# GpSimd adds both halves of the attention mask in every fourth step, TensorE none

## The chip, the cores and the metric

One core of one Trainium2 chip runs the kernel. The metric is the device time of one execution in microseconds (us). Engines in the profile: PE is TensorE's matmul stream and PEld its weight loads, DVE is VectorE, ACT is ScalarE, POOL is GpSimd, SP is SyncE.

## The reference, cut to what matters

`x` is 4096x256, `neigh` 4096x256, `adj` 4096x4096 integers, of which all but a few per row are 0. The output is `x` plus the two halves below.

```python
h = jnp.maximum(_layernorm(x, axis=-1), 0.0)
neib_att = jnp.tanh(neigh @ Wn1 + bn1) @ Wn2 + bn2      # 4096x32
value = neigh @ Wv + bv                                  # 4096x128
x_att = jnp.tanh(h @ Wx1 + bx1) @ Wx2 + bx2              # 4096x32
ws = x_att @ neib_att.T                                  # 4096x4096
ws = jax.nn.leaky_relu(ws, negative_slope=0.01)
ws = jnp.where(adj > 0, ws, -9e15)
agg_neib = jax.nn.softmax(ws, axis=1) @ value
x = x + jnp.concatenate([h @ Wfx + bfx, agg_neib], axis=1)
```

## The kernel before, in words

After a first part that computes `neib_att` and starts `value`, the attention runs in 128 steps. A step s is one chunk of scores: 128 rows of `x` by 1024 neighbours (two PSUM banks of 512). Four chunks make the 4096 neighbours of a tile of rows, four tiles (16 steps) make a group of 512 rows; there are 8 groups. "The step at 5 of a group" is one with s % 16 = 5. Each engine has its own program, written out step by step, and runs it in order; semaphores tie them. The steps of one chunk:

- VectorE, `mask_of` (L680): turns 1024 columns of `adj` into a bf16 mask of 0 or -2^53, two steps ahead, in a ring of three.
- TensorE, `score` (L921, L922): for each half of 512 columns, a matmul of the identity with the mask (L921, which writes the mask into PSUM) and then the matmul of the scores on top of it (L922). From step 19 on (`POOL_MASKS`) the second half has no mask matmul. Before its first matmul it waits for the mask and for `leaked`, the leak of step s - 2, whose PSUM banks it overwrites (L910 to L912).
- ScalarE, `rise` (L552): relu of 99 times the chunk, from PSUM to SBUF.
- GpSimd, in `step` (L438 to L443): from step 19 on, after `rise`, adds the second half of the mask (512 columns) to that result in SBUF.
- VectorE, `leak` (L709): waits for `risen` and `masked`, then adds PSUM and SBUF, times 0.01, which is the leaky relu plus a large negative number where masked, and keeps the running maximum. It is done in VectorE's step s + 1.
- ScalarE, `power` (L564): the exponential of two chunks at once, every second step.

The other half of every step works on the group before, whose weights are ready: two blocks per step, each turned by TensorE (`turn`, L945), copied out rounded by ScalarE (`hi`, L525), its rest computed by VectorE (`lo`, L691), and multiplied with `value` in three matmuls (`product`, L964 to L966). TensorE's `turn` and `product` wait for `lo` of the step before.

The order within a step: TensorE runs both score halves, turn 0, product, turn 1, side work, product. VectorE runs leak(s - 1), lo 0, side work, lo 1, mask_of(s + 2). ScalarE runs hi 0, rise, hi 1, power. GpSimd runs in even steps the load of two chunks of `adj` (`load_adj`, L407, which first waits for VectorE's `mask_done`), then the bias sums of the output (L358, L351), then the mask's add, then the reciprocal root of the variance of the next rows in small operations of 4 columns (`rstd_of`, L369 to L386; steps at 12, 13 and 15 of a group) and their normalisation (`x_normalise`, L391; one each in the steps at 1 and 2, two in the step at 4).

```python
def step(s):            # VectorE, L770
    if s < POOL_MASKS:
        mask_of(s + 2)
    leak(s)             # of chunk s - 1
    lo(s, 0)
    ...
    lo(s, 1)
    if POOL_MASKS <= s < STEPS - 2:
        mask_of(s + 2)
```

Of the kernel before, what the change touches and what calls it, by code (L numbers as in the profile page):

```python
# [29 lines left out]
ALU = mybir.AluOpType  # L30
# [6 lines left out]
BANK = 512  # L37
GROUP = BANK
TILES = GROUP // P
GROUPS = N_X // GROUP  # L40
NEIGH_GROUPS = N_NEIGH // GROUP
CHUNK = 2 * BANK
# [12 lines left out]
MASK_RING = 3  # L55
# [28 lines left out]
V_START, V_STRIDE = 0, 2  # L84
LEFT_0 = 3
POOL_MASKS = BACK_LAG
WARM_UP = 15
NEWTON = 3
NEWTON_OPS = 2 + 4 * NEWTON
# [2 lines left out]
def build(nc, x, adj, neigh, wx1, bx1, wx2, bx2, wn1, bn1, wn2, bn2, wv, bv, wfx, bfx, out):  # L92
    with ExitStack() as ctx:
        def sb(name, shape, dt):
            return ctx.enter_context(nc.sbuf_tensor(name, shape, dt))

        def sem(name):
            return ctx.enter_context(nc.semaphore(name))


        scores = sb("scores", [P, 2 * TILES, N_NEIGH], FP32)
# [4 lines left out]
        mask = sb("mask", [P, MASK_RING, CHUNK], BF16)  # L106
# [90 lines left out]
        masked = sem("masked")  # L197
# [21 lines left out]
        def x_due(s, stage):  # L219

            e = (s - stage) // GSTEPS + 1
            return e if (s - stage) % GSTEPS == 0 and 1 <= e < GROUPS else 0
# [10 lines left out]
        def right_due(s):  # L233

            b = s - FIN_LAG - X_RIGHT
            return b // GSTEPS + 1 if b >= 0 and b % GSTEPS == 0 and b // GSTEPS < GROUPS - 1 else None

        def chunk_of(s):

            return s // GSTEPS % 2, s // CHUNKS % TILES, s % CHUNKS  # L240
# [97 lines left out]
        def _(pool):  # L338
# [8 lines left out]
            def left_sum(e, h):  # L347

                pool.wait_ge(x_left_in, 16 * (e + 1))
                half = x_left.rearrange("p (t d) -> p t d", d=D_OUT)[:, h * TILES // 2:(h + 1) * TILES // 2]  # L350
                pool.tensor_tensor(half, half, b_fx[:, :, :].to_broadcast([P, TILES // 2, D_OUT]), ALU.add).then_inc(  # L351
                    x_summed, 1)

            def right_sum(g, h):

                pool.wait_ge(x_right_in, 16 * (g + 1))
                half = x_right[:, h * TILES // 2:(h + 1) * TILES // 2, :]
                pool.tensor_tensor(half, half, b_v[:, :, :].to_broadcast([P, TILES // 2, D_OUT]), ALU.add).then_inc(  # L358
                    right_summed, 1)

            def rstd_of(e, i):

                done = NEWTON_OPS * e
                if i == 0:
                    pool.wait_ge(aggr_done, e + 1)
                    wait(pool, x_normed, TILES * e)
                    wait(pool, newton, done)
                    pool.sem_inc(pool_joined, 1)
                    pool.tensor_scalar(var_eps[:, :], mean_var[:, :, 1], EPS, None, ALU.add).then_inc(newton, 1)  # L369
                    pool.wait_ge(newton, done + 1)  # L370
                    pool.sem_inc(pool_joined, 1)

                    pool.tensor_scalar(rstd.bitcast(INT32)[:, :], var_eps.bitcast(INT32)[:, :], -0.5,
                                       float(0x5f3759df), ALU.mult, ALU.add).then_inc(newton, 1)
                else:

                    done = done + 2 + 4 * (i - 1)
                    pool.wait_ge(newton, done)
                    pool.tensor_tensor(factor[:, :], rstd[:, :], rstd[:, :], ALU.mult).then_inc(newton, 1)
                    pool.wait_ge(newton, done + 1)  # L380
                    pool.tensor_tensor(factor[:, :], factor[:, :], var_eps[:, :], ALU.mult).then_inc(newton, 1)
                    pool.wait_ge(newton, done + 2)
                    pool.sem_inc(pool_joined, 1)
                    pool.tensor_scalar(factor[:, :], factor[:, :], -0.5, 1.5, ALU.mult, ALU.add).then_inc(newton, 1)
                    pool.wait_ge(newton, done + 3)
                    pool.tensor_tensor(rstd[:, :], rstd[:, :], factor[:, :], ALU.mult).then_inc(newton, 1)  # L386

            def x_normalise(e, i):
                pool.wait_ge(newton, NEWTON_OPS * (e + 1))
                pool.sem_inc(pool_joined, 1)  # L390
                pool.tensor_scalar(x_rows[:, i, :], x_rows[:, i, :], mean_var[:, i, 0:1], rstd[:, i:i + 1],  # L391
                                   ALU.subtract, ALU.mult).then_inc(x_normed, 1)
# [6 lines left out]
            def load_adj(n):  # L399

                tile, c = n // CHUNKS, n % CHUNKS
                if ADJ_RING <= n < ADJ_RING + FRONT:
                    to, ready = adj_front[:, n - ADJ_RING:n - ADJ_RING + LOAD, :], front_ready[(n - ADJ_RING) // LOAD]
                else:
                    i = n % ADJ_RING
                    to, ready = adj_in[:, i:i + LOAD, :], adj_ready[i // LOAD]
                pool.dma_start(to.rearrange("p a n -> p (a n)"),  # L407
                               adj[tile * P:(tile + 1) * P, c * CHUNK:(c + LOAD) * CHUNK]).then_inc(ready, 16)
# [18 lines left out]
            def step(s):  # L427
                n = s + ADJ_RING + (FRONT if s < FRONT else 0)
                if s % LOAD == 0 and n < STEPS and not FRONT <= s < ADJ_RING + FRONT:
                    pool.wait_ge(mask_done, s + LOAD)  # L430
                    load_adj(n)
                for i in range(2):
                    if (g := right_due(s - i)) is not None:
                        right_sum(g, i)
                for i in range(2):
                    if e := x_due(s, X_SUM[i]):
                        left_sum(e, i)
                if POOL_MASKS <= s < STEPS:  # L438

                    parity, tile, c = chunk_of(s)  # L440
                    pool.wait_ge(risen, s + 1)
                    half = scores[:, parity * TILES + tile, c * CHUNK + BANK:(c + 1) * CHUNK]
                    pool.tensor_tensor(half, half, mask[:, s % MASK_RING, BANK:CHUNK], ALU.add).then_inc(masked, 1)  # L443
                for i in range(NEWTON + 1):
                    if e := x_due(s, X_RSTD[i]):
                        rstd_of(e, i)
                for i in range(TILES):
                    if e := x_due(s, X_NORM[i]):
                        x_normalise(e, i)
# [144 lines left out]
        def _(dve):  # L594
# [72 lines left out]
            def mask_of(n):  # L667
# [8 lines left out]
                if n >= MASK_RING:  # L676
                    dve.wait_ge(scored, n - MASK_RING + 1)
                if n - MASK_RING >= POOL_MASKS:
                    dve.wait_ge(masked, n - MASK_RING + 1 - POOL_MASKS)
                dve.tensor_scalar(mask[:, n % MASK_RING, :], source, 0.0, MASKED, ALU.is_le,  # L680
# [13 lines left out]
            def leak(s):  # L694
# [5 lines left out]
                dve.wait_ge(risen, n + 1)  # L700
                if n >= POOL_MASKS:
                    dve.wait_ge(masked, n + 1 - POOL_MASKS)
                if c:
# [66 lines left out]
            def step(s):  # L770
                if s < POOL_MASKS:
                    mask_of(s + 2)
                leak(s)
                lo(s, 0)
                close(s)
                x_work(s)
                negate(s)
                neigh_rest(s)
# [3 lines that stand above are left out]
# [7 lines left out]
        def _(pe):  # L789
# [107 lines left out]

            warm(WARM_UP)
            turn_rows(0, 0)
# [3 lines left out]
            def score(s, h):  # L903

                if s >= STEPS:
                    return
                k = s
                parity, tile, c = chunk_of(s)
                if h == 0:
                    pe.wait_ge(mask_done, k + 1)  # L910
                    if s >= 2:
                        pe.wait_ge(leaked, k - 1)  # L912
                    if s < CHUNKS:

                        pe.wait_ge(att_out, NEIGH_GROUPS - 1 if s == 1 else (s + 1) * CHUNK // GROUP)
                    if tile == 0 and c == 0:
                        pe.wait_ge(x_att, s // GSTEPS + 1)
                half = slice(h * BANK, (h + 1) * BANK)
                on_pool = h == 1 and s >= POOL_MASKS
                if not on_pool:  # L920
                    pe.matmul(ps[:, s % 2, half], ident_bf16, mask[:, s % MASK_RING, half], start=True, stop=False)  # L921
                last = pe.matmul(ps[:, s % 2, half], xs[:, parity, tile * P:(tile + 1) * P],  # L922
                                 neib[:, c * CHUNK + h * BANK:c * CHUNK + (h + 1) * BANK], start=on_pool, stop=True)
                if h == 1:
                    last.then_inc(scored, 1)
# [104 lines left out]
```

## Time and profile before

| what | value |
|---|---|
| median of 3 runs | 500.75 us (500.16 to 500.9) |
| the profiled execution | 500.86 us |
| its span, first to last instruction | 498.9 us |
| PE busy | 472.7 us (95%) |
| PEld busy | 369.5 us (74%) |
| DVE busy | 422.6 us (85%) |
| ACT busy | 420.4 us (84%) |
| POOL busy | 254.4 us (51%) |
| mean granted TensorE clock | 0.995 |
| chain of waits by engine | PE 56%, POOL 15%, issue 11%, ACT 7%, DVE 5%, DMA 4% |

The span is what the profile sees; the execution's own time has 2 us more around it. A matmul's busy time overlaps with its neighbours', so TensorE's share is not a share of its peak. The attention's first scores begin at 35 us and the last at 441; the last group's turns and products follow until the end.

### The profile page before, as it was taken

The page shows a single profiled execution, that of the slowest core. Times are in us where ns is not written, and L with a number is a line of the kernel's source. Part 1 is how long each engine was busy: PE and PEld are TensorE (multiplying, and loading weights), DVE is VectorE, ACT ScalarE, POOL GpSimd, SP SyncE. Part 2 cuts the span into 40 slices and gives each one's busy share as a digit, 9 for nine tenths or more (in the row PEclk, how much of TensorE's full clock was granted, in tenths as well). Part 3 has the DMA queues.
Part 4 walks back from the last instruction along what each step waited for, and adds up shares of the span by engine and source line. Part 5 has one row for each costly group of instructions (what it writes and reads, how often), then busy time and mean ns, then how long its engine had stood idle before and what let it go on. Part 6 is the DMA issues. An engine that isn't in the chain of part 4 may idle for free.

```text
span 498.9 us, 9232 instructions
## 1 busy us (share of the span) xinstructions
PE 472.7 (95%) x3026; PEld 369.5 (74%) x3026; DVE 422.6 (85%) x832; ACT 420.4 (84%) x594; POOL 254.4 (51%) x357
## 2 busy tenths in 40 slices
PE   6998887999999999999999999999999999998996
PEld 5876664677777778777877777777777787766884
DVE  1569888989998999999998999899988999985664
ACT  3564998999989998999999999999899989997552
POOL 1707334646674677557664776477746444430100
PEclk9899999999999999999999999999999999999999
DMA  6793857474458546664567455745675456300100
GB/s 213 200 211 66 194 93 122 79 145 78 82 110 177 95 66 118 116 134 77 106 128 149 77 85 103 168 79 84 106 149 85 81 94 118 69 1 2 42 1 21
DMA packets 36774, 51.41 MB, mean 103 GB/s; under 512 B 3192, under 2 KB 28536, under 8 KB 36728
## 3 DMA queue, kind: packets, MB, share of 16 engines
q0 software_dynamic: 9216, 33.56, 41.4%
q1 hardware_dynamic: 27108, 17.24, 11.3%
q8 instruction: 24, 0.39, 0.3%
q14 instruction: 22, 0.18, 0.1%
q10 hardware_dynamic: 404, 0.03, 0.1%
HBM read 80.19 MB, written 4.19 MB: 169 GB/s over the span
## 4 chain that ended last, share of the span: by engine, by line
PE 56%; POOL 15%; issue 11%; ACT 7%; DVE 5%; DMA 4%; SPq 0%; DVEq 0%; POOLq 0%; ACTq 0%
PE ps_turned L945 15%; PE ps_product L964 8%; PE ps_product L966 7%; PE ps_product L965 7%; PE ps_scores L922 7%; POOL scores L443 7%; PE ps_scores L921 4%; POOL x_rows L391 3%; ACT pt_hi L525 3%; DMA adj_in<-in_adj 2%; POOL adj_in L407 2%; ACT scores L552 2%; ACT scores L564 2%; DMA scores<-in_L_gnn_neigh 2%; DVE pt_lo L691 2%
## 5 line engine op out<-in xcount | busy, mean ns | idle before, releaser
L691 DVE TENSOR_TENSOR pt_lo<-ps_turned,pt_hi 128x512 fp32r<-128x512 f32 x256 | 173.3, 685 | 38.1 <-ACT pt_hi L525 20.2
L525 ACT ACTIVATE pt_hi<-ps_turned 128x512 fp32r<-128x512 f32 x256 | 155.3, 607 | 44.3 <-PE ps_turned L945 43.8
L443 POOL TENSOR_TENSOR scores<-scores,mask 128x512 f32<-128x512 f32 x109 | 127.0, 1165 | 94.2 <-ACT scores L552 93.9
L945 PE MATMUL ps_turned<-ident,scores 128*128 128x128 f32 x1024 | 154.3, 273 | 2.8 <-DVE pt_lo L691 2.4
L945 PEld LDWEIGHTS ps_turned<-ident,scores 128*128 128x128 f32 x1024 | 124.4, 140 | 43.7 <-DVE pt_lo L691 15.1
L552 ACT ACTIVATE scores<-ps_scores 128x1024 f32<-128x1024 f32 x128 | 131.8, 1031 | 11.4 <-PE ps_scores L922 11.4
L564 ACT ACTIVATE scores<-scores,neg_top 128x2048 f32<-128x2048 f32 x64 | 129.0, 2016 | 0.0
L709 DVE CUSTOM_DVE_ANT_0 scores<-ps_scores,scores,top 128x1024 f32<-128x1024 f32 x96 | 122.5, 1276 | 1.7 <-ACT scores L552 1.4
L964 PE MATMUL ps_product<-pt_hi,v_hi 128*128 128x512 f32 x256 | 122.1, 477 | 0.2 <-DVE pt_lo L691 0.2
L922 PE MATMUL ps_scores<-neib,xs 128*128 128x512 f32 x256 | 108.7, 502 | 0.0
L966 PE MATMUL ps_product<-pt_lo,v_hi 128*128 128x512 f32 x256 | 101.4, 396 | 0.0
L965 PE MATMUL ps_product<-pt_hi,v_lo 128*128 128x512 f32 x256 | 100.3, 392 | 0.0
L921 PE MATMUL ps_scores<-mask,ident 128*128 128x512 bf16 x147 | 56.8, 386 | 11.1 <-DVE top L709 8.1
L407 POOL DMA_DIRECT2D adj_in<-in_adj x62 | 36.7, 592 | 55.4 <-DVE mask L680 53.9
L680 DVE TENSOR_SCALAR mask<-adj_in 128x1024 bf16<-128x1024 bf16 x124 | 58.4, 473 | 3.0 <-DMA adj_in<-in_adj 3.0
L966 PEld LDWEIGHTS ps_product<-pt_lo,v_hi 128*128 128x128 f32 x256 | 48.0, 188 | 10.9
L922 PEld LDWEIGHTS ps_scores<-neib,xs 128*128 128x128 f32 x256 | 49.7, 194 | 3.0
L964 PEld LDWEIGHTS ps_product<-pt_hi,v_hi 128*128 128x128 f32 x256 | 48.7, 190 | 2.0 <-issue 1.2
L921 PEld LDWEIGHTS ps_scores<-mask,ident 128*128 128x128 bf16 x147 | 14.3, 97 | 48.0 <-issue 46.8
L965 PEld LDWEIGHTS ps_product<-pt_hi,v_lo 128*128 128x128 f32 x256 | 49.1, 192 | 0.0
L391 POOL TENSOR_SCALAR x_rows<-x_rows,mean_var,rstd 128x256 f32<-128x256 f32 x32 | 40.3, 1261 | 0.5 <-POOL rstd L386 0.2
L709 DVE CUSTOM_DVE_ANT_0 scores<-ps_scores,scores 128x1024 f32<-128x1024 f32 x32 | 38.8, 1214 | 0.1
(76 smaller groups left out, 362.0 us busy)
## 6 DMA issues: line engine op xcount, KB each, us to landing
adj_in<-in_adj POOLq DMA_DIRECT2D x62, 512.0 KB, 5.4
scores<-in_L_gnn_neigh SPq DMA_DIRECT2D x8, 512.0 KB, 5.9
x_rows<-in_x SPq DMA_DIRECT2D x8, 512.0 KB, 6.0
x_left<-in_x SPq DMA_DIRECT2D x8, 256.0 KB, 6.2
x_right<-in_x SPq DMA_DIRECT2D x8, 256.0 KB, 5.1
out_h<-x_left SPq DMA_DIRECT2D x8, 256.0 KB, 2.5
out_h<-x_right SPq DMA_DIRECT2D x8, 256.0 KB, 2.3
scores<-in_adj POOLq DMA_DIRECT2D x2, 512.0 KB, 6.3
```

The source lines that it names most:

```text
L443: pool.tensor_tensor(half, half, mask[:, s % MASK_RING, BANK:CHUNK], ALU.add).then_inc(masked, 1)
L525: act.activation(pt_hi[:, (2 * b + u) % HI_RING], pt[:, u], ACT.Copy).then_inc(hi_done, 1)
L552: act.activation(scores[:, parity * TILES + tile, c * CHUNK:(c + 1) * CHUNK], ps[:, s % 2], ACT.Relu, scale=RISE).then_inc(risen, 1)
L564: act.activation(cols, cols, ACT.Exp, bias=neg_top[:, tile % 2, :], accum_out=sums[:, parity, tile, c // 2:c // 2 + 1]).then_inc(exp_done, 1)
L691: dve.tensor_tensor(pt_lo[:, u], pt[:, u], pt_hi[:, (2 * b + u) % HI_RING].bitcast(FP32), ALU.subtract).then_inc(lo_done, 1)
L709: dve.tensor_tensor_reduce(cols, ps[:, n % 2], cols, SLOPE, start, ALU.add, ALU.max, top[:, tile % 2, c:c + 1]).then_inc(leaked, 1)
L921: pe.matmul(ps[:, s % 2, half], ident_bf16, mask[:, s % MASK_RING, half], start=True, stop=False)
L922: last = pe.matmul(ps[:, s % 2, half], xs[:, parity, tile * P:(tile + 1) * P], neib[:, c * CHUNK + h * BANK:c * CHUNK + (h + 1) * BANK], s ...
L945: last = pe.transpose(pt[:, u, i * P:(i + 1) * P], scores[:, parity * TILES + i, n * P:(n + 1) * P], ident[:, :])
L964: pe.matmul(acc, v_hi[:, n, :], pt_hi[:, b2_ % HI_RING, :], start=n == 0, stop=False)
L965: pe.matmul(acc, v_lo[:, n, :], pt_hi[:, b2_ % HI_RING, :], start=False, stop=False)
L966: pe.matmul(acc, v_hi[:, n, :], pt_lo[:, b2_ % 2, :], start=False, stop=n == BLOCKS - 1).then_inc(block_used, 1)
```

## The change

From step 21 to step 125, in every step with s % 4 = 1, GpSimd adds all 1024 columns of the mask in one instruction where it added 512, and TensorE leaves out its one remaining mask matmul (L921); the first half's score matmul then starts its PSUM bank itself. The waits and their places are as before.

```diff
@@ constants
 POOL_MASKS = BACK_LAG
+BOTH_EVERY, BOTH_AT = 4, 1
@@ helpers
+        def both_on_pool(s):
+
+            return s >= POOL_MASKS and s % BOTH_EVERY == BOTH_AT
+
@@ gpsimd, step
                     pool.wait_ge(risen, s + 1)
-                    half = scores[:, parity * TILES + tile, c * CHUNK + BANK:(c + 1) * CHUNK]
-                    pool.tensor_tensor(half, half, mask[:, s % MASK_RING, BANK:CHUNK], ALU.add).then_inc(masked, 1)
+                    first = 0 if both_on_pool(s) else BANK
+                    cols = scores[:, parity * TILES + tile, c * CHUNK + first:(c + 1) * CHUNK]
+                    pool.tensor_tensor(cols, cols, mask[:, s % MASK_RING, first:CHUNK], ALU.add).then_inc(masked, 1)
@@ tensor, score
-                on_pool = h == 1 and s >= POOL_MASKS
+                on_pool = h == 1 and s >= POOL_MASKS or both_on_pool(s)
```

## Rows read from the trace of the kernel before

**Rows 1.** Busy time by stretch, one group of 16 steps: PE, PEld, DVE, ACT, POOL, clock.

```profile
299.80:352.80 53.00, 52.61 (x325) 41.11 (x324) 49.85 (x101) 49.35 (x70) 34.42 (x47) 1.00 0.59 110
```

**Rows 2.** The chain of waits, 336 to 340 us: start us, us on the chain, what.

```profile
336.32 0.23 PE ps_scores L921
...
337.63 0.60 ACT pt_hi L525
338.23 0.93 ACT scores L552
...
339.22 1.17 POOL scores L443
```

**Rows 3.** Page, costliest groups: the mask matmul; line view of L443: ns min/median/max.

```profile
L921 PE MATMUL ps_scores<-mask,ident 128*128 128x512 bf16 x147 | 56.8, 386 | 11.1 <-DVE top L709 8.1
...
L443 POOL TENSOR_TENSOR scores<-scores,mask x109: 1152/1165/1183, 87.5 to 444.1; 128x512 f32<-128x512 f32 x109
```

**Rows 4.** GpSimd's groups by shape: busy us, mean ns, idle before.

```profile
L351 POOL TENSOR_TENSOR x_left<-x_left,b_fx 128x256 f32<-128x256 f32 x16 | 11.8, 742 | 0.2
L379 POOL TENSOR_TENSOR factor<-rstd 128x4 f32<-128x4 f32 x24 | 5.7, 236 | 1.0
...
L381 POOL TENSOR_TENSOR factor<-factor,var_eps 128x4 f32<-128x4 f32 x24 | 5.1, 213 | 1.9
```

**Rows 5.** Timeline, add and leak of step 81, score(83): start us, us, [idle before].

```profile
292.94 1.17 POOL L443 TENSOR_TENSOR scores<-scores,mask 128x512 f32<-128x512 f32 x1 [1.34 <-ACT scores L552]
...
294.85 1.27 DVE L709 CUSTOM_DVE_ANT_0 scores<-ps_scores,scores,top 128x1024 f32<-128x1024 f32 x1
...
296.39 0.39 PE L921 MATMUL ps_scores<-mask,ident 128*128 128x512 bf16 x1
```

**Rows 6.** Timeline, GpSimd's queue and leak of step 85, score(87).

```profile
304.84 2.43 POOL L391 TENSOR_SCALAR x_rows<-x_rows,mean_var,rstd 128x256 f32<-128x256 f32 x2
...
307.24 1.17 POOL L443 TENSOR_TENSOR scores<-scores,mask 128x512 f32<-128x512 f32 x1
...
308.78 1.27 DVE L709 CUSTOM_DVE_ANT_0 scores<-ps_scores,scores,top 128x1024 f32<-128x1024 f32 x1
...
310.34 0.39 PE L921 MATMUL ps_scores<-mask,ident 128*128 128x512 bf16 x1
```

**Rows 7.** Timeline, add of step 89, leaks of steps 89 and 90, score(92).

```profile
319.63 1.17 POOL L443 TENSOR_TENSOR scores<-scores,mask 128x512 f32<-128x512 f32 x1 [1.33 <-ACT scores L552]
...
321.64 1.28 DVE L709 CUSTOM_DVE_ANT_0 scores<-ps_scores,scores,top 128x1024 f32<-128x1024 f32 x1
...
325.36 1.28 DVE L709 CUSTOM_DVE_ANT_0 scores<-ps_scores,scores,top 128x1024 f32<-128x1024 f32 x1
...
326.81 0.39 PE L921 MATMUL ps_scores<-mask,ident 128*128 128x512 bf16 x1
```

**Rows 8.** Timeline, adds and leaks of steps 93 and 94, scores (95) and (96).

```profile
328.49 0.57 POOL L407 DMA_DIRECT2D adj_in<-in_adj  x1 [1.01 <-DVE mask L680]
...
333.19 1.17 POOL L443 TENSOR_TENSOR scores<-scores,mask 128x512 f32<-128x512 f32 x1
...
334.57 1.27 DVE L709 CUSTOM_DVE_ANT_0 scores<-ps_scores,scores,top 128x1024 f32<-128x1024 f32 x1
...
336.16 0.39 PE L921 MATMUL ps_scores<-mask,ident 128*128 128x512 bf16 x1
...
337.17 1.16 POOL L443 TENSOR_TENSOR scores<-scores,mask 128x512 f32<-128x512 f32 x1
...
338.64 1.28 DVE L709 CUSTOM_DVE_ANT_0 scores<-ps_scores,scores,top 128x1024 f32<-128x1024 f32 x1
...
340.08 0.39 PE L921 MATMUL ps_scores<-mask,ident 128*128 128x512 bf16 x1
```

**Rows 9.** Adjacency load's landing (page, DMA issues); timeline, an add and a mask operation.

```profile
adj_in<-in_adj POOLq DMA_DIRECT2D x62, 512.0 KB, 5.4
...
343.68 1.18 POOL L443 TENSOR_TENSOR scores<-scores,mask 128x512 f32<-128x512 f32 x1
...
344.25 0.91 DVE L680 TENSOR_SCALAR mask<-adj_in 128x1024 bf16<-128x1024 bf16 x1
```

## The prediction

> **What bounds the kernel now.** I read the profile from the whole to the single step. The busy time by stretch comes first: over one group of 16 steps (299.8 to 352.8 us) TensorE is busy 52.61 of 53.0 us, VectorE 49.85, ScalarE 49.35 and GpSimd 34.42, at a granted TensorE clock of 1.00 [rows 1]. GpSimd looks like the engine with room. A busy TensorE is not yet a bound, so the chain of waits comes next: its pieces on TensorE follow each other without a hole, and a mask matmul (L921) takes 0.23 us of it, though its row says 391 ns, because matmuls overlap. The same chain then leaves TensorE, and this is what matters here: at 337.63 it goes over ScalarE's hi copy (L525) and relu (L552) to GpSimd's add (L443, 339.22, 1.17 us) [rows 2]. So two paths are tied: TensorE's own stream, and the loop score(s) on TensorE, relu on ScalarE, add on GpSimd, leak on VectorE, score(s+2) on TensorE (score(s+2) overwrites the scores' bank that leak(s) reads).
>
> The counts: 147 mask matmuls, 109 half-width adds from 87.5 to 444.1 us, one step per 3.30 us (356.6 / 108) [rows 3].
>
> **What is removed.** Steps 21, 25, ... 125 change, 27 of them; in a group they are those at 1, 5, 9 and 13, steps 81, 85, 89, 93 in the group that I follow. Each loses one mask matmul: 27 x 0.23 = 6.2 us of TensorE's stream. The load of its weights lies beside other matmuls and counts nothing.
>
> **What is added.** Each of the 27 adds has 1024 columns, not 512. The trace has no add so wide, so I bound it. Doubling everything gives 1165 ns more. From below: the 256-column add of line 351 takes 742 ns, the 512-column one 1165; 423 ns for 256 columns makes 0.85 us for 512 more. (Line 351 adds float to float with a repeated bias, so it is not quite the same kind.) The 4-column adds take 213 to 236 ns [rows 4], and how much of that is paid once, and not by the column, no row tells; I put it at 65 ns, near nothing, because the same instruction at 512 columns is the nearest row. That gives the value I use, **+1.10 us**. The Trainium skill (GPSIMD Engine Reference, on elementwise cost) gives 4497 ns for a float add of 2048 columns; half of it, an estimate, is 2.25 us for 1024, 1.08 more than the row of 512, and the sum below would be some 0.5 us less by it.
>
> **What hides it.** The question is how late leak(s) becomes and what stands behind it. VectorE runs, in order: lo, mask(s+2), leak(s), lo, ... ; an add that ends late holds leak(s), and behind it both lo's of the next step, their mask and leak(s+1); TensorE's turns and products wait on lo, its score(s+2) on leak(s). Two floors are needed. From the end of an add to the start of its leak: 0.21 us (334.36 to 334.57, step 93). From the end of a leak to TensorE's score two steps on: 0.16 us (339.92 to 340.08, step 94) [rows 8]. What exceeds a floor is slack. Now the lateness against the times of before, carried through one group, with the 0.23 us credited where ScalarE's relu, not GpSimd's queue, releases the add:
>
> Step 81 [rows 5]: the add waited for the relu (1.34 us idle), so it ends 1.10 - 0.23 = 0.87 late. Slack to leak: 294.85 - 294.11 - 0.21 = 0.53, so leak is 0.34 late. Slack to score(83): 296.39 - 296.12 - 0.16 = 0.11. Score(83) is **0.23 late**.
>
> Step 85 [rows 6]: the add has no idle before it; it stands behind two normalisations (2.43 us) and the add of step 84, so TensorE's 0.23 earlier is worth nothing. Their chain starts 0.23 late, the add ends 0.23 + 1.10 = 1.33 late. Slack to leak 308.78 - 308.41 - 0.21 = 0.16: leak 1.17 late. Slack to score(87) 0.29 - 0.16 = 0.13: **1.04 late**.
>
> Step 89 [rows 7]: released by the relu again: 1.04 - 0.23 + 1.10 = 1.91. Slack 321.64 - 320.80 - 0.21 = 0.63: leak 1.28 late. VectorE is full from there to leak(90), which is 1.28 late too, and score(92) has 326.81 - 326.64 - 0.16 = 0.01 of slack: **1.27 late**.
>
> Step 93 [rows 8]: GpSimd's queue begins with the adjacency load (L407), which waits for VectorE's mask, 1.28 late. Behind it GpSimd is full until add(93), which ends 1.28 + 1.10 = 2.38 late. Slack to leak is 0: 2.38, score(95) 2.22. Add(94) stands in the same queue, with the small operations and a load between (0.17 us may be given back): 2.21, slack to leak(94) 338.64 - 338.33 - 0.21 = 0.10: 2.11, and score(96) has no slack: **2.11 late**, where the next group begins.
>
> So a group costs 2.1 us, the removed matmuls already counted in. Steps 33 to 109 are five such groups of four: 10.5 us. The seven others (21 to 29, 113 to 125) I take at half the price, 0.26 each, 1.8 us, since the last group has no normalisations or loads of the next rows in GpSimd's queue. The sum is **+12.3 us**. The profiled execution took 500.86 us (span 498.9), 0.1 above the median of 500.75; the forecast is 513.0.
>
> Costed at nothing: the adjacency load behind a longer add. It lands 5.4 us after issue [rows 9]; issued at 328.49 it is there at 333.9, and its first use is the mask ahead of leak(94) at 338.64, some 4 us later; 1.1 us fits. If that cover went, VectorE would wait in L680. VectorE's mask operation itself is held while GpSimd adds: one that began at 344.25 inside an add took 0.91 us and ended 0.30 after the add did (345.16 against 344.86) [rows 9]. Under a double add this holds each time, but the leak behind it waits for the same add and starts 0.21 after its end as before; price zero.
>
> With +0.85 for the add the same steps give 1.13 a group and 6.6 us in all (507.4); with +1.165, 2.39 and 14.1 (514.9).
>
> **Rivals.**
> (1) *Faster: TensorE's stream is the only bound.* All lateness would be taken up in VectorE's idle time, 3.15 us of each group [rows 1], and 6.2 us come off: 494.6. For it: the unbroken TensorE pieces in the chain. Against: step 93 has no slack to leak and 0.16 to the score. It decides where the wider add costs less than about 0.4 us more (0.16 of slack plus the 0.23 saved), and the lowest bound is 0.85. Chance 0.11.
> (2) *No change: VectorE is the bound and has room for the waits.* VectorE is busy 94% of the group, TensorE's weight loads 78% (41.11 of 53.0) [rows 1]; if TensorE were not what binds, the removed matmul gives nothing and the late adds fall into the same 3.15 us: 500.9. The pieces 0.23 us apart [rows 2] speak against it. The Trainium skill (Perfetto Trace Analysis, Identifying the Most-Contended Engine) says just this, that TensorE is to be judged by its weight loads and MFU, VectorE by occupancy; by that rule the change relieves the wrong engine. Chance 0.05.
> (3) *A smaller loss.* Lateness carried over a group is partly given back, since some of VectorE's 3.15 us lies between a late leak and the next lo. With three quarters given back at the lowest price of the add: some 2 us, 503. This is the low side of my forecast, not a case by itself.
> (4) *A larger loss: the lock works the other way too.* If the double add, or the one after it, starts behind VectorE's mask operation, GpSimd waits the 0.3 us instead: 27 x 0.3 = 8.1 us more, 521. Against: of 109 adds none took over 1183 ns [rows 3]. Chance 0.07.
>
> **The numbers.** The forecast, with its low and high sides, has 0.77, rival 4 0.07, so slower is 0.84, faster 0.11, same 0.05. About 0.2% is what a measurement of this kernel can tell from no change. The range goes from 503 (rival 3) to 518 (the +1.165 end, 514.9, and part of rival 4).
>
> **What would show it.** Right: 82 adds of 1165 ns and 27 near 2.27 us, 120 mask matmuls; in the steps at 5 and 13 of a group leak starts 0.2 us after the double add ends, and VectorE shows idle time there ended by GpSimd; TensorE waits for leak(s) two steps on, about 1 us after the steps at 5 and 13 and little after those at 1 and 9; a group takes 55.1 us instead of 53; GpSimd's add has a clearly larger share of the chain. Wrong: an add of 1024 columns under 1.6 us; TensorE's scores evenly 3.25 us apart; or the clock below 1.00 in the waits, which would add a cost that is not in my sum.

## The result: 1.9% slower, and the profile after

| | before | changed |
|---|---|---|
| median | 500.82 us (4 runs, 500.16 to 501.64) | 509.70 us (4 runs, 508.55 to 510.39) |
| ratio, 95% interval | | 1.019 (1.0164 to 1.0216) |
| span | 498.9 us | 507.3 us |
| chain of waits | PE 56%, POOL 15%, ACT 7%, DVE 5% | PE 38%, POOL 22%, ACT 12%, DVE 8% |

The two medians alone give 1.018, inside the interval. Two executions at a lower granted clock are left out of the medians below: one of the eighth kernel (534.4 us, clock 0.851) and one of the tenth (523.36 us, 0.979).

In the changed kernel's code the lines have moved by five or six: the add is L449, the mask matmul L927, the scores' matmul L928, the mask operation L686, the leak L715. The page's busy line and its rows for the mask matmul and the mask operation:

```profile
PE 471.7 (93%) x2966; PEld 366.8 (72%) x2999; DVE 440.3 (87%) x832; ACT 419.3 (83%) x594; POOL 282.4 (56%) x357
...
L686 DVE TENSOR_SCALAR mask<-adj_in 128x1024 bf16<-128x1024 bf16 x124 | 77.2, 624 | 2.7 <-DMA adj_in<-in_adj 2.7
...
L927 PEld LDWEIGHTS ps_scores<-mask,ident 128*128 128x128 bf16 x120 | 11.6, 97 | 54.2 <-issue 52.8
```

GpSimd's groups by shape, changed kernel (busy us, mean ns, idle before):

```profile
L449 POOL TENSOR_TENSOR scores<-scores,mask 128x512 f32<-128x512 f32 x82 | 95.5, 1165 | 63.0 <-ACT scores L558 62.5
L449 POOL TENSOR_TENSOR scores<-scores,mask 128x1024 f32<-128x1024 f32 x27 | 58.1, 2151 | 17.0 <-ACT scores L558 16.9
```

The change did what it says: 27 wide adds, and 120 loads of the identity for mask matmuls where there were 147. (The matmul row of L927 lists fewer than its loads; the trace misses some.) The wide add takes 2151 ns, 0.99 us more than the narrow one, not 1.10.

The same group of 16 steps as before, busy time by stretch, from score(80) to score(96):

```profile
292.60:347.40 54.80, 52.73 (x316) 40.83 (x321) 53.11 (x101) 49.27 (x70) 38.55 (x47) 1.00 0.57 107
```

The group is 1.8 us longer than 53.0 [rows 1], TensorE's clock is still 1.00, and VectorE is now listed as the busiest engine (53.11 us). That last reading is a trap, as the timeline of the step at 13 shows (step 93, changed kernel; start us, us, idle before):

```profile
339.73 2.15 POOL L449 TENSOR_TENSOR scores<-scores,mask 128x1024 f32<-128x1024 f32 x1
...
340.74 1.43 DVE L686 TENSOR_SCALAR mask<-adj_in 128x1024 bf16<-128x1024 bf16 x1
...
341.83 0.39 POOL L384 TENSOR_TENSOR factor<-rstd 128x4 f32<-128x4 f32 x1
...
342.08 1.27 DVE L715 CUSTOM_DVE_ANT_0 scores<-ps_scores,scores,top 128x1024 f32<-128x1024 f32 x1
...
343.51 0.38 PE L927 MATMUL ps_scores<-mask,ident 128*128 128x512 bf16 x1 [0.63 <-DVE top L715]
```

The wide add ends at 341.88. The mask operation (0.42 us when it waits for nothing) is listed as busy for 1.43 us and ends at 342.17, 0.29 after the add; the leak starts 0.20 after the add; score(95) has waited 0.63 us for it. So the wait for GpSimd is there, but it is booked as VectorE's work: all VectorE's extra busy time (422.6 to 440.3 us) is in L686, whose 124 operations take 77.2 us where they took 58.4.

Where in the group the time is lost, from the starts of the scores in the changed kernel:

```profile
292.66 0.38 PE L927 MATMUL ps_scores<-mask,ident 128*128 128x512 bf16 x1
...
302.07 0.38 PE L927 MATMUL ps_scores<-mask,ident 128*128 128x512 bf16 x1 [0.16 <-DVE top L715]
...
316.68 0.38 PE L927 MATMUL ps_scores<-mask,ident 128*128 128x512 bf16 x1 [0.53 <-DVE top L715]
...
333.34 0.39 PE L927 MATMUL ps_scores<-mask,ident 128*128 128x512 bf16 x1
...
347.43 0.38 PE L927 MATMUL ps_scores<-mask,ident 128*128 128x512 bf16 x1
...
401.24 0.39 PE L927 MATMUL ps_scores<-mask,ident 128*128 128x512 bf16 x1
```

Those are score(80), (83), (87), (92), (96) and (112); score(95) is in the fence before. The kernel before has score(80) and score(112) at

```profile
287.06 0.39 PE L921 MATMUL ps_scores<-mask,ident 128*128 128x512 bf16 x1
...
393.25 0.39 PE L921 MATMUL ps_scores<-mask,ident 128*128 128x512 bf16 x1
```

and the others in [rows 5 to 8]. Lateness since score(80), changed less before:

| score | wide add two or three steps earlier | measured | forecast (add +1.10) | the same steps with +0.99 |
|---|---|---|---|---|
| 83 | at 1 | 9.41 - 9.33 = 0.08 | 0.23 | 0.12 |
| 87 | at 5 | 24.02 - 23.28 = 0.74 | 1.04 | 0.81 |
| 92 | at 9 | 40.68 - 39.75 = 0.93 | 1.27 | 0.93 |
| 95 | at 13 | 50.85 - 49.10 = 1.75 | 2.22 | 1.76 |
| 96 | at 13, through add(94) | 54.77 - 53.02 = 1.75 | 2.11 | 1.65 |

The steps at 5 and 13 cost 0.66 and 0.82 us, those at 1 and 9 0.08 and 0.19.

### The profile page after: what moved, and what is told of

It reads as the page before. It is cut to its first block, busy times and chain, and to the rows that moved or that the text cites. A ratio compares the mean times of both kernels' runs of the same rounds, so it can differ in the third digit from the quotient of the medians.

```text
span 507.3 us, 9145 instructions
## 1 busy us (share of the span) xinstructions
PE 471.7 (93%) x2966; PEld 366.8 (72%) x2999; DVE 440.3 (87%) x832; ACT 419.3 (83%) x594; POOL 282.4 (56%) x357
## 4 chain that ended last, share of the span: by engine, by line
PE 38%; POOL 22%; issue 14%; ACT 12%; DVE 8%; DMA 4%; SPq 0%; DVEq 0%; POOLq 0%; ACTq 0%
PE ps_turned L951 11%; POOL scores L449 10%; POOL x_rows L396 7%; PE ps_scores L928 5%; PE ps_product L970 5%; PE ps_product L972 5%; PE ps_product L971 5%; ACT pt_hi L531 4%; ACT scores L570 4%; ACT scores L558 3%; DVE pt_lo L697 3%; DVE mask L686 3%; DMA adj_in<-in_adj 2%; POOL adj_in L412 2%; DMA scores<-in_L_gnn_neigh 2%
## 5 line engine op out<-in xcount | busy, mean ns | idle before, releaser
L449 POOL TENSOR_TENSOR scores<-scores,mask 128x512 f32<-128x512 f32 (+1 forms) x109 | 153.6, 1409 | 79.9 <-ACT scores L558 79.4
L715 DVE CUSTOM_DVE_ANT_0 scores<-ps_scores,scores,top 128x1024 f32<-128x1024 f32 x96 | 122.3, 1274 | 1.9 <-ACT scores L558 1.4
L928 PE MATMUL ps_scores<-neib,xs 128*128 128x512 f32 x256 | 104.2, 485 | 6.7 <-DVE top L715 5.5
L686 DVE TENSOR_SCALAR mask<-adj_in 128x1024 bf16<-128x1024 bf16 x124 | 77.2, 624 | 2.7 <-DMA adj_in<-in_adj 2.7
L928 PEld LDWEIGHTS ps_scores<-neib,xs 128*128 128x128 f32 x256 | 48.3, 191 | 4.5 <-issue 0.5
L927 PEld LDWEIGHTS ps_scores<-mask,ident 128*128 128x128 bf16 x120 | 11.6, 97 | 54.2 <-issue 52.8
L927 PE MATMUL ps_scores<-mask,ident 128*128 128x512 bf16 x87 | 33.3, 382 | 13.3 <-DVE top L715 11.0
L396 POOL TENSOR_SCALAR x_rows<-x_rows,mean_var,rstd 128x256 f32<-128x256 f32 x32 | 41.9, 1312 | 0.5 <-POOL rstd L391 0.2
L715 DVE CUSTOM_DVE_ANT_0 scores<-ps_scores,scores 128x1024 f32<-128x1024 f32 x32 | 38.9, 1214 | 0.1
```

What stands on the lines that cost most here:

```text
L449: pool.tensor_tensor(cols, cols, mask[:, s % MASK_RING, first:CHUNK], ALU.add).then_inc(masked, 1)
L715: dve.tensor_tensor_reduce(cols, ps[:, n % 2], cols, SLOPE, start, ALU.add, ALU.max, top[:, tile % 2, c:c + 1]).then_inc(leaked, 1)
```

## The experiments

Theory A is the one of the prediction: a wide add costs what it exceeds of the slack in its own place. Theory B is the main rival now that the kernel was slower: each wide add costs a third of a microsecond wherever it stands (8.9 us / 27). A third question is how the gain on TensorE and the loss through GpSimd add up. All ratios are to the kernel before.

**1 and 2. Other places for the wide adds.**

```diff
-BOTH_EVERY, BOTH_AT = 4, 1
+BOTH_EVERY, BOTH_AT = 4, 3      # second kernel: 4, 0
```

> The wide adds stand in the steps with s % 4 = 3 (28 of them) instead of s % 4 = 1. Theory A (a wide add costs what it exceeds of the slack of its own step: from the add's end to leak, from leak to the score two steps on): at 3 and 15 of a group there is 0.8 us of slack before leak, at 7 there is 0.67 between leak and score, at 11 0.4 and 0.27, and no step has the GpSimd queue late, so nearly nothing is lost: 499 to 503 us. Theory B (each wide add costs its 0.33 us wherever it stands, by GpSimd's share of the SBUF port or by its work): 28 x 0.33, 510 us.

> The wide adds stand in the steps with s % 4 = 0 (27). Theory A: at 0 and 12 of a group the add already starts late in GpSimd's queue and leak has no slack (0.8 and 1.0 us), at 4 and 8 some 0.2 us, and the add at 5 is pushed behind two normalisations by it: about 2.5 us a group, 515 us. Theory B: 27 x 0.33, 510 us.

Measured: 506.51 us for the steps with s % 4 = 3, ratio 1.0116 (1.0096 to 1.0135); 522.86 us for s % 4 = 0, ratio 1.0445 (1.0422 to 1.0467). Place decides: 28 wide adds cost 5.4 us (501.08 before), 27 cost 21.8. Theory B falls. Theory A had the order right, the sizes not: 506.5 lies 3.5 us above its range, 522.9 is 7.9 above its value. The trace of the first kernel shows what was left out, at the wide add of step 79 (15 of its group) and behind it (GpSimd's timeline, then the starts of score(81) and score(82) on TensorE's):

```profile
289.09 2.15 POOL L449 TENSOR_TENSOR scores<-scores,mask 128x1024 f32<-128x1024 f32 x1 [0.67 <-ACT scores L558]
291.20 0.38 POOL L384 TENSOR_TENSOR factor<-rstd 128x4 f32<-128x4 f32 x1
...
293.79 0.61 POOL L412 DMA_DIRECT2D adj_in<-in_adj  x1
294.43 1.18 POOL L449 TENSOR_TENSOR scores<-scores,mask 128x512 f32<-128x512 f32 x1
...
292.96 0.39 PE L927 MATMUL ps_scores<-mask,ident 128*128 128x512 bf16 x1
...
297.19 0.38 PE L927 MATMUL ps_scores<-mask,ident 128*128 128x512 bf16 x1 [0.67 <-DVE top L715]
```

The wide add does not hurt its own leak. It holds eight small operations, a load's issue and add(80) in GpSimd's queue. They follow each other with pauses of 0.2 us at most until add(80), which starts at 294.43; leak(80) comes after it, and score(82) starts 4.23 us after score(81) where it took 3.4 before. I had carried lateness through GpSimd's queue in the prediction, but left it out of these two expectations.

For the second kernel this is not the whole account. Its groups from score(48) to score(96) last 55.9 us each, 2.6 to 2.9 more than before where 2.5 was expected. The one from score(96) to score(112) lasts 58.77, 5.6 more, and holds one mask operation of 3.40 us (the tenth kernel, below, shows what that is):

```profile
399.26 3.40 DVE L686 TENSOR_SCALAR mask<-adj_in 128x1024 bf16<-128x1024 bf16 x1
```

**3 and 4. One cause taken away: a shorter queue ahead of the wide add at 5.**

```diff
-X_NORM = (1, 2, 4, 4)
+X_NORM = (1, 2, 3, 4)      # in the changed kernel, and in the kernel before
```

> The changed kernel with the third of the four normalisations moved from the step at 4 of a group to the step at 3, so that one and not two stand before the wide add of the step at 5. Theory A: that add then starts with its relu, 0.8 us earlier, its leak is hardly late, and a group gets 0.8 us shorter: 505 us. Theory B: no change, 509.7 us.

> The kernel before with the same move of one normalisation. Theory A: the add at 5 had 0.16 us of slack before leak and leak 0.13 before the score, so an earlier add gains nothing: 500.8 us, within 0.5. Theory C (the move itself is what helps, not through the wide add): as much gain here as in the changed kernel, about 496 us.

Measured: 505.70 us, ratio 1.0102 (1.0082 to 1.0122), in the changed kernel; 500.25 us, ratio 0.9983 (0.9957 to 1.0008), in the kernel before. Four of the 8.9 us are gone, and the move by itself has no effect that can be told from none. The add at 5 in the third kernel (step 85):

```profile
308.06 1.22 POOL L396 TENSOR_SCALAR x_rows<-x_rows,mean_var,rstd 128x256 f32<-128x256 f32 x1
309.56 2.15 POOL L449 TENSOR_TENSOR scores<-scores,mask 128x1024 f32<-128x1024 f32 x1 [0.28 <-ACT scores L558]
...
312.00 1.27 DVE L715 CUSTOM_DVE_ANT_0 scores<-ps_scores,scores,top 128x1024 f32<-128x1024 f32 x1
```

GpSimd is now idle 0.28 us before it and is released by the relu: the queue was the cause at 5, as the prediction's step for 85 says.

**5 and 6. Half of the change each.**

```diff
-            return s >= POOL_MASKS and s % BOTH_EVERY == BOTH_AT
+            return s >= POOL_MASKS and s % GSTEPS in (1, 9)      # sixth kernel: (5, 13)
```

> Wide adds (and no mask matmul) only in the steps at 1 and 9 of a group, 13 of them. Theory A, with the wide add measured at 2.15 us (0.99 more): both start with their relu and have 0.5 to 0.6 us of slack before leak; the step at 1 makes a group 0.1 us later, that at 9 another 0.1 to 0.2: 502 us (0.2 to 0.4% more than before). Theory B (each wide add costs 0.33 us wherever it stands): 13 x 0.33, 505.2 us.

> Wide adds only in the steps at 5 and 13 of a group, 14 of them. Theory A: both add starts stand in GpSimd's queue, so the matmul left out gives nothing back and 0.99 us meets 0.3 and 0.2 us of slack; a group gets 1.4 us longer, the whole 7 to 8 us: 508 us. Theory B: 14 x 0.33, 505.5 us.

Measured: 502.31 us, ratio 1.0038 (1.0017 to 1.0059); 509.04 us, ratio 1.0180 (1.0138 to 1.0222). Theory B's 505.2 and 505.5 would be 1.009 and 1.0096 and lie outside both intervals. The two losses, 0.4% and 1.8%, add up to about the whole, and fourteen of the 27 wide adds carry nearly all of it.

**7 and 8. The two halves of each edit.**

```diff
@@ seventh kernel, gpsimd
-                    first = 0 if both_on_pool(s) else BANK
+                    first = BANK
@@ eighth kernel, tensor
-                on_pool = h == 1 and s >= POOL_MASKS or both_on_pool(s)
+                on_pool = h == 1 and s >= POOL_MASKS
```

> The mask matmul is left out in the 27 steps but GpSimd's add stays 512 columns wide, so the first half of those chunks gets no mask. Theory A: TensorE's stream gets 0.93 us shorter a group, of which the loop over ScalarE, GpSimd and leak lets about half through: 2 to 4 us less than before, 497 to 499. Theory D (TensorE is the only bound once the wide add is away): 6.2 us less, 494.6.

> GpSimd adds both halves in the 27 steps and TensorE keeps its mask matmul, so the first half is masked twice there, which leaves the exponential at 0. Theory A: the whole 0.99 us counts in every one of the steps, by my steps 2.1 us a group where the changed kernel has 1.6: 511.5 to 513 us. Theory B (costs just add up): the changed kernel plus what the run without the wide add gains.

Measured: 497.87 us, ratio 0.9946 (0.9929 to 0.9964), without the wide adds; 513.17 us, ratio 1.0245 (1.0207 to 1.0284), with the matmuls kept. (Of the eighth kernel only the time is used here.) The matmuls taken out are worth 2.8 us, under half of the 6.2 that the chain of waits gave them (27 x 0.23). This is what two tied paths would do: TensorE's gets shorter, and the other lets no more through. No run takes the other path away, so that part is argued. The group shows it, from score(80) to score(96) in the seventh kernel 336.70 - 284.21 = 52.49 us, 0.5 us shorter than before, not 0.93:

```profile
284.21 0.38 PE L927 MATMUL ps_scores<-mask,ident 128*128 128x512 bf16 x1
...
336.70 0.38 PE L927 MATMUL ps_scores<-mask,ident 128*128 128x512 bf16 x1
```

The wide adds alone cost 12.5 us (513.2 less 500.7). 12.5 less 2.8 is 9.7, the change itself 8.9: plain addition is off by little, so these two kernels do not tell theory A's account from it.

**9. The correction of theory A tested: the first of these kernels less the wide adds at 15.**

```diff
-            return s >= POOL_MASKS and s % BOTH_EVERY == BOTH_AT
+            return s >= POOL_MASKS and s % GSTEPS in (3, 7, 11)
```

> As the run with the wide adds at 3, 7, 11 and 15 of a group, less those at 15 (21 wide adds). That run showed the group 1.05 us longer, with 0.8 of it in one place: the step at 1 lasted 4.2 us, since the wide add at 15 pushed the eight small operations, the load and the add of the step at 0 back by 1 us in GpSimd's own queue. Theory A': slack is to be counted through GpSimd's queue as well as to leak; without 15 the group is within 0.25 us of before: 500 to 502.5 us. Theory B' (each of them costs its share, 5.4 us / 28): 21 x 0.19, 504.8 us.

Measured: 501.66 us, ratio 1.0026 (1.0008 to 1.0044). Taking seven wide adds away brought 4.4 of 5.4 us back (each against the kernel before as timed beside it, 501.08 and 500.63); 504.8 would be 1.0083. What stands behind the add in GpSimd's own queue is part of the slack.

**10. A miss: GpSimd's queue relieved further.**

```diff
@@ on the third kernel
-X_LEFT_LOAD, X_SUM = 13, (12, 14)
-X_RIGHT = 8
+X_LEFT_LOAD, X_SUM = 13, (10, 11)
+X_RIGHT = 6
```

> The changed kernel with the third normalisation at 3 of a group, and the bias sums of the output, which stood ahead of the adds of the steps at 12, 13 and 14, done in the steps at 10 and 11. Theory A: the wide add at 13 starts about 0.5 us earlier against leak, the group gets 0.5 us shorter than with the normalisation alone (505.7): 503 us. Theory E (what holds the wide add at 13 is the load that waits for VectorE's mask, not the sums): 505.7, no change.

Measured: 515.38 us (three runs, 512.28 to 517.25), ratio 1.0309 (1.0279 to 1.0339), 12 us above my number. The groups are unlike each other; the starts of score(64), score(80) and score(96):

```profile
238.54 0.39 PE L927 MATMUL ps_scores<-mask,ident 128*128 128x512 bf16 x1
...
294.37 0.39 PE L927 MATMUL ps_scores<-mask,ident 128*128 128x512 bf16 x1
...
347.69 0.39 PE L927 MATMUL ps_scores<-mask,ident 128*128 128x512 bf16 x1
```

The second lasts 53.32 us, where the third kernel's was 54.14 (290.19 to 344.33): this is the relief I wanted, even more than the 0.5 us. The first lasts 55.83. Its steps 74 and 75 in the timeline:

```profile
275.29 0.73 POOL L356 TENSOR_TENSOR x_left<-x_left,b_fx 128x256 f32<-128x256 f32 x1
275.98 1.16 POOL L449 TENSOR_TENSOR scores<-scores,mask 128x512 f32<-128x512 f32 x1
277.11 0.72 POOL L363 TENSOR_TENSOR x_right<-x_right,b_v 128x256 f32<-128x256 f32 x1
277.79 0.73 POOL L356 TENSOR_TENSOR x_left<-x_left,b_fx 128x256 f32<-128x256 f32 x1
278.49 1.15 POOL L449 TENSOR_TENSOR scores<-scores,mask 128x512 f32<-128x512 f32 x1
...
276.84 3.09 DVE L686 TENSOR_SCALAR mask<-adj_in 128x1024 bf16<-128x1024 bf16 x1
279.85 1.27 DVE L715 CUSTOM_DVE_ANT_0 scores<-ps_scores,scores,top 128x1024 f32<-128x1024 f32 x1
```

The mask operation began during add(74), which ended at 277.14, and leak(74) was ready to go from then. It came through only at 279.93, 0.29 after the last of a train of GpSimd operations without a pause between them. Moving the sums had made that train. But a train does not always do this. In step 58 of the same kernel the same operations stand in the same order, and the mask operation came through at the first boundary, 0.29 us after the add's end; there GpSimd's next operation took 0.93 us instead of 0.72:

```profile
222.67 1.16 POOL L449 TENSOR_TENSOR scores<-scores,mask 128x512 f32<-128x512 f32 x1
223.79 0.93 POOL L363 TENSOR_TENSOR x_right<-x_right,b_v 128x256 f32<-128x256 f32 x1
...
222.92 1.20 DVE L686 TENSOR_SCALAR mask<-adj_in 128x1024 bf16<-128x1024 bf16 x1
```

In the profiled execution, the shortest of this kernel's, the step at 10 has such a hold in three groups (3.07, 3.09 and 3.9 us, steps 42, 74 and 106) and none in two (steps 58 and 90). The three groups with a hold last 55.8 us each, the two without 53.9 and 53.3, so a hold costs its group some 2 to 2.5 us. Against the third kernel the three groups are 6.0 us longer together, and the whole span is 6.7 longer (510.3 against 503.6): in this execution the holds account for the loss. What decides between a hold and none no trace shows. That the longer executions have more holds fits their scatter, but they have no trace.

**11 and 12. A version that beats both?**

```diff
@@ eleventh kernel; the twelfth has the edits of the tenth besides
-            return s >= POOL_MASKS and s % BOTH_EVERY == BOTH_AT
+            return s >= POOL_MASKS and s % GSTEPS in (3, 7)
```

> Wide adds only in the steps at 3 and 7 of a group (14), where nearly all of the 0.99 us is covered. Theory A: nothing lost at 3, at 7 some 0.1 us, against 0.46 us of TensorE a group of which about half comes through: 499 to 500.5 us, no difference or up to 0.3% faster.

> Both: GpSimd's queue relieved as in the run before this one, wide adds only in the steps at 3 and 7 of a group. Theory A: the relief alone gained nothing in the kernel before (0.9983 with an interval that holds 1), the two steps little: 498.5 to 500 us, at most 0.5% faster than before.

Measured: 500.11 us, ratio 0.9984 (0.9971 to 0.9996), and 509.05 us, ratio 1.0167 (1.014 to 1.0194). Fourteen wide adds, in the two best places, are free and bring 0.16%, less than the 0.2% that a measurement here can tell for sure. The twelfth missed in the same way: its trace has holds of 3.09 and 3.59 us. The two groups that they stand in are 6.5 us longer together than in the eleventh; the span is 9.7 longer, and the other 3.2 us are not explained.

## Why the prediction was right, and where its sizes were off

It forecast 513.0 (503 to 518), 2.4% slower; measured 509.7.

- *The wide add*: forecast +1.10 us, measured +0.99. Between the rows of 256 and 512 columns (+0.85) and plain doubling (+1.165), the truth lay about in the middle; I leaned too far towards doubling. With 0.99 the prediction's own steps give 1.65 us for the group, measured 1.75. The estimate that it took from the Trainium skill (GPSIMD Engine Reference, on elementwise cost), half of a 2048-column add, was 2.25 us; the row is 2.15. (A slip in its upper end changes nothing: with +1.165 its steps give 2.37 us a group and 13.9 in all, not 2.39 and 14.1.)
- *Step by step*: four of the five latenesses in the table agree with the corrected steps within 0.07 us. The costly places are 5 and 13, as forecast, and the third kernel and the pair (1, 9) against (5, 13) show it by taking them away. Of the giving back that rival 3 asks for, the group shows none.
- *Five groups at the full price*: this is the term that failed. The four groups from score(32) to score(96) lost 6.7 us together (219.14 against 212.41), 1.7 each. The fifth, from score(96) to score(112), lost 0.64 us (53.81 against 53.17), not 2.1. GpSimd computes the reciprocal roots of a group's rows well ahead, those for the last group in steps 92 to 95. In steps 108 to 111 its queue therefore has none, and the add of step 109 starts with its relu. I had seen that such work is missing for the last group and not for the one before it.

```profile
393.45 2.15 POOL L449 TENSOR_TENSOR scores<-scores,mask 128x1024 f32<-128x1024 f32 x1 [0.20 <-ACT scores L558]
```

- *The seven others*: forecast 1.8 us. What is left of the span's 8.4 us, after 6.7 and 0.64, is 1.05.
- *TensorE's matmuls*: I credited 0.23 us only where the relu releases the add. The seventh kernel bears that out: 2.8 of 6.2 us arrive. Rival 1 (494.6) is excluded even without the wide adds. So is rival 2, by which TensorE's matmuls would be worth nothing.
- *The signs to look for*: the 82 and 27 adds, the 120 mask matmuls, and the leak 0.2 us behind the wide add came as said. TensorE's waits came at the places named, but smaller, 0.53 and 0.63 us where I said about 1. One sign was wrong: I looked for idle time of VectorE ended by GpSimd, and it shows as busy time in L686.
- *Rival 4*, that GpSimd would be held as well, has nothing for it in the adds: 2151 ns on average (2.13 to 2.17 us). It seems held in the operation behind the add instead: the small one at 341.83 took 0.39 us where most of its kind take 0.20, as it did in the kernel before (0.38 at 334.33).
- *The held mask operation*, priced at zero: right under a single add. The leak starts 0.20 or 0.21 us after 26 of the 27 wide adds (0.55 at step 109), in the steps at 1 and 9 too. That holding can last over a train of operations was in none of my cases, though the kernel before has a short one. There a mask operation waited past the end of an add (384.58) and of the bias sum behind it (385.27), to 385.56:

```profile
384.25 1.31 DVE L680 TENSOR_SCALAR mask<-adj_in 128x1024 bf16<-128x1024 bf16 x1
```

Left open: how much of each loss is the leak's own wait for the add and how much the mask operation's, which stands ahead of the leak in VectorE's queue. Both come right behind the add: the leak starts 0.20 us after it and the mask operation ends 0.29 us after it. At step 126 of the kernel before no mask operation stands ahead, and the leak starts at 443.17, 0.18 us after an add that ended at 442.99; with one it is 0.21. That bounds the difference at some 0.03 us in an ordinary step.

## What to carry to other kernels

An engine that is half idle on average may have no room at all in a given step: add up, for each step, the slack (time to spare) to the consumer, the slack from there to the bound engine, and what stands behind in the engine's own queue. Work moved off the bound engine is worth only what the next tied path lets through, here under half. Before spreading a change over every fourth step, read which fourth: the same edit cost 1.2%, 1.9% or 4.5% by its phase, and nothing at two chosen places.

## What the runs showed of the hardware

- VectorE's bf16 mask operation (0.42 us) does not run beside a GpSimd add of two tensors. It ends 0.28 to 0.30 us after the add (in 38 of 44 cases in the changed kernel; 0.53 to 0.55 in five, 0.97 in one), and its wait is booked as its own busy time: 1.43 us under a wide add. Beside GpSimd's normalisation, which reads one tensor, it waited less in the kernel before: begun at 305.01, 0.17 us after the normalisation, it took 0.65 us and ended while that was still running.
- With GpSimd's operations back to back it is served at the first boundary in some cases and passed over in others: at three boundaries in steps 42 and 74 of the tenth kernel (3.07 and 3.09 us), at none in its step 58 (1.20 us). Where it is served, GpSimd's next operation is the one that waits (0.93 us instead of 0.72). The Trainium skill (SBUF — State Buffer, Who interferes with whom) says of VectorE's modes that use two ports, and with them the pair of SBUF ports that it shares with GpSimd: the engine that issues first has that pair for the whole instruction, and the other is fully blocked. The single adds agree (blocked to their end), the trains go beyond it, and no run here shows which mode the mask operation uses.
- A GpSimd add of float and bf16 to float takes 1165 ns for 512 columns and 2151 ns for 1024. From these two widths, an estimate is 1.93 ns a column and 0.18 us once.
